# Self attention of a decoder layer: values made once, global queries' product moved, third part of queries and keys on GpSimd

## The reference, cut to what matters

```python
x = x + attn(layernorm(x))
q, k, v = (split_heads(h @ W + b) for ...)          # 16 heads of 8
scores = einsum('bhqd,bhkd->bhqk', q, k) / sqrt(8)
scores = where(mask, scores, -inf)                   # blocks of 64 tokens, and 8 global tokens
out = einsum('bhqk,bhkd->bhqd', softmax(scores), v) @ Wo + bo
```

## Time and profile before

| | us |
|---|---|
| median of 3 runs (lowest, highest) | 609.08 (607.75, 611.74) |
| span of the profiled execution | 640.0 |
| busy in that span: TensorE, VectorE | 515.9, 420.0 |
| busy in that span: GpSimd, ScalarE | 314.7, 300.4 |
| the 16 bodies of the self attention | about 34 to 271 |

### The profile page before, as it was taken

One profiled execution on the slowest core, in us unless ns is written; L12 is line 12 of the kernel. 1 busy time (PEld: TensorE's weight loads), 2 busy tenths in 40 slices (PEclk: granted clock), 3 DMA queues, 4 the chain that ended last, 5 costly groups with the idle time before them and its releaser, 6 DMA issues. The chain is left out here.

```text
span 640.0 us, 17229 instructions
## 1 busy us (share of the span) xinstructions
PE 515.9 (81%) x5995; PEld 380.8 (59%) x5995; DVE 420.0 (66%) x1241; ACT 300.4 (47%) x756; POOL 314.7 (49%) x612
## 2 busy tenths in 40 slices
PE   2879899898889889779999989897579867778710
PEld 2656666676666666456776766665347656656510
DVE  8558788898877778779997987874343222333227
ACT  2745555556556654335654555544214232332327
POOL 4644333433334342111677787777744456556530
PEclk9979899899989999869997998999799799999875
DMA  6442322333333444225232322221044223233139
GB/s 171 100 113 62 68 50 64 94 90 99 92 93 99 102 109 104 60 62 122 68 84 76 96 78 79 80 66 35 32 129 109 78 81 88 74 86 88 42 123 299
DMA packets 96004, 58.33 MB, mean 91 GB/s; under 512 B 24560, under 2 KB 92224, under 8 KB 95920
## 3 DMA queue, kind: packets, MB, share of 16 engines
q1 hardware_dynamic: 80928, 42.95, 26.2%
q0 software_dynamic: 4576, 9.91, 4.7%
q10 hardware_dynamic: 10416, 4.39, 2.8%
HBM read 20.83 MB, written 17.50 MB: 60 GB/s over the span
## 5 line engine op out<-in xcount | busy, mean ns | idle before, releaser
L645 POOL DMA_INDIRECT expert_out<-ey,xt x79 | 76.5, 968 | 66.2 <-DVE ey L1097 45.7
L748 DVE TENSOR_REDUCE nmax<-ps 128x8 f32<-128x512 f32 x128 | 85.3, 684 | 19.0 <-PE ps L1520 13.9
L1222 ACT ACTIVATE probs<-ps 128x512 f32<-128x512 f32 x128 | 75.1, 605 | 17.7 <-PE ps L1726 13.0
L534 POOL TENSOR_SCALAR pgq<-pgq,gstat 128x256 f32<-128x256 f32 x16 | 16.7, 1043 | 132.7 <-DVE gstat L812 132.7
L1092 DVE TENSOR_TENSOR eh<-ps,sg 128x256 f32<-128x256 f32 x40 | 17.0, 425 | 81.6 <-issue 43.6
L578 POOL DMA_INDIRECT expert_in<-xn,sloti x52 | 54.9, 1056 | 19.0 <-issue 8.6
L1932 PE MATMUL ps<-kbd,turned 128*128 x160 | 26.5, 289 | 25.3 <-ACT turned L1405 15.5
L1520 PE MATMUL ps<-kbd,qs 96*64 96x128 bf16 x512 | 38.5, 293 | 9.2 <-DMA qs<-part 8.0
L1405 ACT COPY turned<-ps 128x512 f32<-128x512 f32 (+1 forms) x43 | 23.8, 554 | 41.8 <-PE ps L1917 20.3
L1924 PE MATMUL ps<-wgu,turned 128*128 x160 | 41.7, 384 | 1.1 <-issue 1.1
L689 DVE TENSOR_SCALAR xn<-x_rows,mv,rstd 128x128 f32<-128x128 f32 x64 | 27.2, 476 | 23.1 <-POOL rstd L488 23.0
(11 more groups left out here) (237 smaller groups left out, 1392.6 us busy)
## 6 DMA issues: line engine op xcount, KB each, us to landing
kbd<-part SPq DMA_DIRECT2D x192, 32.0 KB
qs<-part SPq DMA_DIRECT2D x96, 64.0 KB
xt<-expert_in SPq DMA_DIRECT2D x80, 72.0 KB
qs<-part ACTq DMA_DIRECT2D x48, 64.0 KB
ck_scr<-wgu SPq DMA_DIRECT2D x6, 512.0 KB
ckbd<-ck_scr SPq DMA_DIRECT2D x16, 192.0 KB
kbd<-part SPq DMA_DIRECT2D x48, 64.0 KB
wgu<-in_L_ffn_gate_up_w SPq DMA_DIRECT2D x4, 512.0 KB, 4.0
```

What stands on the lines that cost most here:

```text
L645: pool.indirect_dma_start(ys, bass.IndirectOffsetOnAxis(xt[p][:, E:E + 1].bitcast(I32), 0), ey[q % 4][:, j, :], None).then_inc(e_(f"out{q ...
L748: v.tensor_reduce(nmax[:, u, 8 * half:8 * half + 8], bank[:, :].rearrange("p (h k) -> p h k", k=64), AX.X, ALU.max, negate=True).then_inc( ...
L1222: a_.activation(probs[:, 2 * i:2 * i + 2, :], P2[i % 2][:, :].rearrange("p (j q) -> p j q", j=2), ACT.Exp, scale=SCALE).then_inc(s("probs" ...
```

## The change

Four things, all in the self attention:

- Values: the doubled copy `xnT2` is gone, so `self_columns` makes one copy. `self_values` on TensorE makes the values once, in two products of 128 tokens. ScalarE makes `vbd` from them in eight copies of half the size: for each half `a` of the destination's partitions and each half `i` of the source's, two copies, and where `a` and `i` differ the copy goes across partitions. `vtok` becomes one copy of 128 partitions. Semaphores follow (`values_ps` for `vdup_ps` and `xnT` for `xnT2`, `vtok` counts one for each sequence).
- The global queries' product stands between head pairs 1 and 2, where it stood ahead of pair 0.
- `self_last_part(b + 1)` goes from VectorE to GpSimd, behind `self_global_heads(b + 1)` and ahead of the scaling of `pgq`. The third part of sequence 0, ahead of the loop, stays on VectorE.
- A wait of ScalarE for `values_ps` ahead of the first columns of the cross attention.

```diff
-        xnT2 = sb("xnT2", [128, NB, 2, BLOCK])
+            def self_last_part(b):
+                pool.wait_ge(s_("part"), 3 * b + 2)
+                g.tensor_tensor(part[:, 2, :], res[:, :], part[:, 1, :], ALU.subtract).then_inc(s_("part"), 1)
             def self_body(b, p):
                 if has(b + 1):
                     self_global_heads(b + 1, 1 - p)
+                    self_last_part(b + 1)
...
-                if has(b + 1):
-                    self_last_part(b + 1)
-                elif CROSS and b + 1 == B:
+                if CROSS and b + 1 == B:
                     cross_last_part(0)
...
             def self_columns(b):
                 act.wait_ge(s_("xT_ps"), b + 1)
-                at_least(act, s_("vdup_ps"), b)
+                at_least(act, s_("values_ps"), b)
                 at_least(act, s_("xg"), b)
-                a_.copy(xnT2[:, :, :, :], A0[:, 0:S].rearrange("p (n k) -> p n k", n=NB).unsqueeze(2).to_broadcast([128, NB, 2, BLOCK])).then_inc(s_("xnT2"), 1)
                 a_.copy(xnT[:, :], A0[:, 0:S]).then_inc(s_("xnT"), 1)
...
             def self_values(b, p):
-                act.wait_ge(s_("vdup_ps"), b + 1)
-                value_cells(a_, vbd[p][:, :, :, :], A1, s_("vbd"))
+                act.wait_ge(s_("values_ps"), b + 1)
+                for a in range(2):
+                    for i in range(2):
+                        src = A1[64 * i:64 * i + 64, 0:2 * E].rearrange("p (u g jj a d) -> p u g jj a d", u=2, jj=2, a=2, d=D)[:, :, :, :, a, :]
+                        to = vbd[p][64 * a:64 * a + 64, i::2, :, :].rearrange("p u (g jj) c -> p u g (jj c)", jj=2)
+                        for jj in range(2):
+                            cell = jj * 48 + a * D
+                            last = a_.copy(to[:, :, :, cell:cell + D], src[:, :, :, jj, :])
+                    last.then_inc(s_("vbd"), 1)
             def self_rows(b, p):
-                for i in range(2):
-                    h = slice(64 * i, 64 * i + 64)
-                    a_.copy(vtok[p][h, :, :], A1[h, :].rearrange("p (u i c) -> p u i c", u=2, i=2)[:, :, i, :]).then_inc(s_("vtok"), 1)
+                a_.copy(vtok[p][:, :, :], A1[:, 0:2 * E].rearrange("p (u c) -> p u c", u=2)).then_inc(s_("vtok"), 1)
...
             def self_values(b):
-                pe.wait_ge(s_("xnT2"), b + 1)
+                pe.wait_ge(s_("xnT"), b + 1)
                 at_least(pe, s_("vg"), b)
-                for n in range(NB):
-                    last = mm(A1[:, n * E:(n + 1) * E], xnT2[:, n, :, :].rearrange("p a k -> p (a k)"), wv[:, :], start=True, stop=True)
-                last.then_inc(s_("vdup_ps"), 1)
+                for u in range(2):
+                    last = mm(A1[:, u * E:(u + 1) * E], xnT[:, u * 128:(u + 1) * 128], wv[:, :], start=True, stop=True)
+                last.then_inc(s_("values_ps"), 1)
...
                 if has(b):
-                    global_queries(b, p)
                     for i in range(4):
+                        if i == 2:
+                            global_queries(b, p)
                         pair(b, p, i)
```

More of the change, by code:

```diff
@@ L1278, in self_body @@
                         act.wait_ge(s_("xg"), B)
+                        act.wait_ge(s_("values_ps"), B)
                     cross_start(b + 2 - B)
@@ L1498, in self_values @@
             def self_values(b):
-                pe.wait_ge(s_("xnT2"), b + 1)
+                pe.wait_ge(s_("xnT"), b + 1)
                 at_least(pe, s_("vg"), b)
-                for n in range(NB):
-                    last = mm(A1[:, n * E:(n + 1) * E], xnT2[:, n, :, :].rearrange("p a k -> p (a k)"), wv[:, :], start=True, stop=True)
-                last.then_inc(s_("vdup_ps"), 1)
+                for u in range(2):
+                    last = mm(A1[:, u * E:(u + 1) * E], xnT[:, u * 128:(u + 1) * 128], wv[:, :], start=True, stop=True)
+                last.then_inc(s_("values_ps"), 1)
             def self_global_values(b):
                 pe.wait_ge(s_("vbd"), 2 * b + 2)
-                pe.wait_ge(s_("vtok"), 2 * b + 2)
+                pe.wait_ge(s_("vtok"), b + 1)
                 pe.wait_ge(s_("xg"), b + 1)
```

## The result

| kernel | median of the runs | lowest to highest | profiled execution: time, span |
|---|---|---|---|
| before | 608.53 us (14 runs) | 605.88 to 613.52 | 608.64, 606.8 (profiled again beside the experiments) |
| after | 611.68 us (14 runs) | 606.76 to 614.73 | 611.28, 609.4 |

After against before is 1.0054, with a 95% interval of 1.0028 to 1.0079: about 3 us slower, where 603.9 was forecast and the range ended at 608.5. The difference is small, but its interval leaves out 1, and it has the other sign.

What follows compares the result with a forecast made beforehand. Two nearly equal chains bound a body: copies 14.31 us, engines 13.6. Third-part waits 3.1, first part's lateness 0.8 and first body 1.3 summed to 5.2 us, 609.08 to 603.9; range 597.0 to 608.5.

Steps and rivals of the forecast that it cites:

- I take that VectorE wins: Shared port at the spread: VectorE's two copies go before GpSimd's third part; otherwise a wait of up to 0.9 us.
- Rival B: GpSimd wins the port at the spread: VectorE loses 0.9 us, about 2.5 us gained in all, 606.6; chance 0.20.
- engines' chain: Self-attention body from values over global queries, pairs, exponentials and `pgq` to the maxima: 13.6 us, shortened by 0.7.
- copies' chain: Self-attention body from one rest over SyncE's nine issued copies and the scores to the next rest: 14.31 us, length kept.
- The 3.1 us of waits for the third part: SyncE's queue waiting for VectorE's third part in 3 bodies: all 3.1 us go.
- The 0.8 us for the first part's lateness: First part's six copies in SyncE's queue: 0.1 us won in each of 8 bodies, bounds 0 to 4.8.
- Values once: Ahead of the pairs: TensorE 0.53 us less a body, ScalarE net 0.5 less, crossing partitions taken as free.
- Queries' product between the pairs: TensorE between pairs 1 and 2: pair 0 gains 0.44 us, cost nothing, or up to 0.6 on pair 2.
- The engines' chain at 12.9: Self-attention body over the engines, without waits for copies: 12.9 us in place of 13.6.
- Rival A: Profile stretches the copies, so engines bind unprofiled: each body gains 0.7 us, 11.1 in all, 598.0; chance 0.25.
- Rival C: TensorE's clock falls more often through longer waits ahead of the scores: 7.6 us slower, 616.7; chance 0.08.
- D: Nothing on the path: waits for the third part become waits for landings, only the first body gains, 607.8; chance 0.05.

Runs made afterwards that it cites:

- e3: After, with GpSimd's third part waiting also for the last copy of VectorE's spread; 604.18 us, 0.9926 of before.
- e1: After with the third part back on VectorE in its old place; 605.31 us, 0.9947 of before.
- e5: Before with only the values made once; 605.41 us, 0.9958 of before.
- e10: Before with the queries' product between pairs 1 and 2 and the third part on GpSimd behind the spread; 607.01 us, 0.9986 of before.
- e4: Before with only the third part moved to GpSimd, waiting for the spread's last copy; 609.99 us, 1.0018 of before.
- e11: Before with only the third part moved to GpSimd behind the spread, that same kernel measured again; 607.20 us, 1.0013 of before.
- e0: The kernel before, unchanged, profiled again; 608.64 us, span 606.8 us.
- e6: After with GpSimd's third part waiting for the spread, and GpSimd instead of SyncE issuing that part's three copies; 594.84 us, 0.9777 of before.
- e8: After, third part behind the spread, GpSimd issuing its three copies and ScalarE the second part's two query copies; 604.93 us, 0.9962 of before.

## Why the prediction was wrong, by its own steps

- **"I take that VectorE wins."** This is the step that failed. The prediction had the rule right (who starts first keeps the other out, and the earlier trace rows), but applied it to the pair of copies as if it were one instruction: "its first copy is 0.2 us ahead". The two are excluded instruction by instruction, and GpSimd only has to start before the *second* copy does. The rows said so: the second part was ready at 141.89, half of the two copies was over at 142.07, and GpSimd starts 0.08 us after its input. Measured, the second copy took 1.25 to 1.88 us in 13 bodies, for 0.41. The Trainium skill (SBUF — State Buffer, "Who interferes with whom") says that the lock is kept for a whole instruction. The trace agrees as far as it can be read: the second copy begins 0.07 us behind GpSimd and ends 0.28 us behind GpSimd's end. The records of GpSimd and of the *first* copy overlap by 0.15 us (0.28 in some bodies) and neither is longer than alone, so the edges of the records don't show the lock exactly.
- **Rival B** was thus the case, with its price too low. VectorE lost 0.97 us (0.9 forecast) and gained 0.68. The engines' chain became 8.67 - 0.07 + 5.30 = 13.9 us, from 8.31 - 0.07 + 5.30 = 13.54 (13.6 forecast). I held 13.8, or 14.1, to be hidden under the copies' 14.31. That length was read from one body, and it holds a long issue:

```profile
146.55 1.07 SPq L382 DMA_DIRECT2D kbd<-part  x1
```

Without its 0.46 us over the usual 0.61 the copies' chain is 13.85 us long, and 13.85 is the body of e3, in which the copies decide. So the collision made the engines' chain about as long as the copies' and left nothing to hide it under. B's gain of 2.5 us didn't come. That the time is 3 us *over* before is not explained by this, as the bodies are no longer than before's.
- **The 3.1 us of waits for the third part**, the largest term of the sum, was mis-sized as well: it is one execution's. Before profiled again has 1.6 us, e1 1.4, and after 1.1, so 0.5 us went. The 0.8 us for the first part's lateness isn't seen either: the fourteen bodies are 0.3 us shorter, where 3.9 were forecast.
- **A wait that I didn't list:** pair 1 waits for L798, the maximum behind the spread, because its bank holds the global scores. So a late VectorE stops TensorE for 1.11 us before pair 1 and not only at `pgq`, and what pair 0 wins (it starts 1.43 us behind the turn, for 2.31 before) is lost.
- **Values once** at TensorE: 0.61 us for 1.06, -0.45 (-0.53 forecast). ScalarE's crossing copies: eight in 1.30 us (1.64 at most forecast, nothing for crossing). Both right. Alone they came out at 2.6 us (e5), with an interval from 0.7 to 4.4, where I gave 1.3 for the first body. First body: 15.83 us for 16.86, -1.0 (-1.3 forecast).
- **Queries' product between the pairs:** cost nothing, and gave nothing (e10, e1).
- **The third part's duration** was 1.16 us (1.2 forecast).
- **The engines' chain at 12.9** is what e3 has: 7.70 - 0.07 + 5.30 = 12.93. And the scores' wait rose to 0.83 (0.7 to about 1.3 forecast), so that "the engines' 0.7 us mostly turns into a longer wait" was right, for the kernel in which the collision is gone. e3's 604.18 us lies at the forecast 603.9. That is luck in part: only half of the sum's largest term was there to be had, and e4 and e11, which by the sum should have had it, had no gain in time.
- **Rival A** fell with e0: nothing is stretched by the profile. **Rival C** isn't seen in the bodies: TensorE's clock was at the lower level for 3.4 us of the fourteen, 10.2 and 13.7 in the two profiles of before, and the body with a wait of 1.53 us ahead of the scores kept a clock of 1.00. What C cites from the Trainium skill (TensorE: Matmul & The Clock Gate, "HAM oscillation — how this bites in real kernels") is told of a kernel whose waits for DMA are longer than the 0.7 to 1.5 us that after has, so it didn't make C the rule. Nor did the body of 17.6 us cost 3.2 us by its clock alone: its scores waited 1.74 us for copies. Over the whole kernel the mean granted clock of the timed runs was 0.935 in after and 0.937 in the runs of before beside e1 to e3; at 3.3 us for 0.01 that is 0.7 of the 3 us. **D** has the sum of the bodies right (the first gains 1.0 us, the others 0.3 together) and not the reason: the way from turn to `global_query_turn` got longer and used up the waits.

## What to carry to other kernels

Before an operation moves to GpSimd, list every VectorE instruction that can start within its duration, one by one: a group of two short copies has a gap into which a long GpSimd instruction slips, and the second copy then pays nearly all of it. If that lies on a chain, tie GpSimd's start to the end of the short ones; one wait was worth 1.3% here. And before a wait in a profile becomes a term of a sum, see whether a second profile of the same kernel has it: here 3.1 us were 1.6. And where a queue issues fifteen small copies a body, moving two or three to another engine's queue took 8 to 9 us off e3 (1.3 to 1.5%), more than any work taken from the engines did, as long as what the freed queue issues next doesn't run ahead of the last copy.

## What was unexpected of the hardware

- The two copies of one loop, back to back on VectorE, are open in the middle to a GpSimd instruction. It started 0.07 or 0.20 us ahead of the second, and 0.41 us turned to 1.25 to 1.38. A memset of GpSimd stood right behind it in three bodies: in two the copy waited for that too (1.88 us), in one the copy came first (1.36) and the memset took 0.87 us for 0.58.
- ScalarE reading the upper 64 partitions and writing the lower ones, or the other way round, costs nothing extra: eight 64 x 64 copies, four of them crossing, in 1.30 us, 0.16 each. The crossing ones have records of 203 to 209 ns and the others of 189 to 217.
- GpSimd issues a copy in 0.54 to 0.86 us (0.56 in the median), about as long as SyncE (0.57 to 0.7 for most, 0.62 in the median, and 1.0 to 1.8 for a few). The last of its three copies lands after 3.0 us in the median in e6, and after up to 6.0 us in e8; in the body shown, with a 512 KB transfer issued just ahead, it was 4.8.
